# Down product of a two-stage expert network cut into chunks of 128 and 64 rows, five matmuls per tile instead of six

## The reference

```python
# layer 0: 64 experts, top 8 of 64 per token, softmax weights
gate = ragged_dot(hidden_sorted, gate_proj_w, group_sizes)      # 512 -> 192
up   = ragged_dot(hidden_sorted, up_proj_w, group_sizes)        # 512 -> 192
out  = ragged_dot(silu(gate) * up, down_proj_w, group_sizes)    # 192 -> 512
# layer 1: 48 experts kept of 128, top 8, at most 192 tokens per expert
g, u = split(einsum('ech,eoh->eco', xb, gate_up_proj), 2)
out  = einsum('eci,ehi->ech', silu(g) * u, down_proj)           # 192 -> 512
```

## Time and profile before

| | |
|---|---|
| median of 3 executions | 2465.17 us |
| the profiled execution | 2475.7 us |
| its span, first to last instruction | 2474.0 us |
| mean granted TensorE clock | 0.872 |
| first expert stage, first to last down product | 608.6 to 1284.6 us |
| second expert stage | 1985.2 to 2409.5 us |
| TensorE busy over the span | 1874.6 us, 76% |
| VectorE busy | 1669.7 us, 67% |
| GpSimd busy | 1318.0 us, 53% |
| ScalarE busy | 730.4 us, 30% |

### The profile page before, as it was taken

The page is one execution under the profiler, slowest core; times in us unless marked ns, Lnnn a source line. Parts: engine busy times, 40 slices in busy tenths (PEclk is TensorE's granted clock), DMA queues, the critical chain, the costliest instruction groups (busy, mean ns, idle before and its releaser), DMA issues. The chain is left out here.

```text
span 2474.0 us, 36661 instructions
## 1 busy us (share of the span) xinstructions
PE 1874.6 (76%) x9110; PEld 1485.2 (60%) x9111; DVE 1669.7 (67%) x2703; ACT 730.4 (30%) x1434; POOL 1318.0 (53%) x847
## 2 busy tenths in 40 slices
PE   6797969233999999999974979595702199999990
PEld 3464545122989988989973555353401188888880
DVE  5659676742767777777742276979697187787764
ACT  2121212001434444444432233333321034433440
POOL 2313656745777777777762000534343666677770
PEclk9898979565999999999996989798955599999995
DMA  6001021013887888888965102020100379988975
GB/s 237 17 18 51 1 68 35 1 64 94 208 216 196 219 230 220 233 227 231 243 123 198 34 1 85 0 85 1 52 0 34 100 201 235 239 228 227 241 157 209
DMA packets 126505, 325.18 MB, mean 131 GB/s; under 512 B 26636, under 2 KB 27148, under 8 KB 125042
## 3 DMA queue, kind: packets, MB, share of 16 engines
q0 software_dynamic: 68912, 124.93, 24.8%
q1 hardware_dynamic: 55426, 195.44, 23.9%
q10 hardware_dynamic: 2112, 4.19, 0.4%
HBM read 242.90 MB, written 99.45 MB: 138 GB/s over the span
## 5 line engine op out<-in xcount | busy, mean ns | idle before, releaser
L91 POOL DMA_INDIRECT tab_rows<-pair,slot x256 | 317.0, 1238 | 210.4 <-issue 101.7
L954 POOL DMA_INDIRECT xg<-x_rows,ids x270 | 374.0, 1385 | 100.3 <-issue 82.2
L83 PE MATMUL gu<-wgu_h,xgT_h 128*128 x1040 | 377.1, 363 | 6.5 <-DVE wgu_l L1108 2.7
L83 PE MATMUL gu<-wgu_l,xgT_h 128*128 x1040 | 354.5, 341 | 0.0
L83 PE MATMUL gu<-wgu_h,xgT_l 128*128 x1040 | 351.6, 338 | 0.0
L963 POOL DMA_INDIRECT acc_rows<-ysb,ids x128 | 228.2, 1783 | 129.5 <-DMA acc_rows<-ysb,ids 72.5
L963 POOL DMA_INDIRECT odd_rows<-ysb,ids x128 | 236.3, 1846 | 91.5 <-ACT ysb L1006 29.5
L1006 ACT ACTIVATE ysb<-yp,wts 128x512 f32<-128x512 f32 x256 | 176.5, 689 | 289.1 <-PE yp L83 240.4
L1123 DVE TENSOR_TENSOR xgT_l<-tpx,xgT_h 128x512 fp32r<-128x512 f32 x262 | 179.5, 685 | 110.8 <-ACT xgT_h L992 98.4
L83 PE MATMUL yp<-wd_h,hT_h 96*128 x512 | 222.6, 435 | 2.4 <-DVE hT_l L1131 1.9
L1108 DVE TENSOR_TENSOR wgu_l<-wgu_sb,wgu_h (+1 forms) x112 | 196.9, 1758 | 40.6 <-issue 39.8
(11 more groups left out here) (333 smaller groups left out, 3659.1 us busy)
## 6 DMA issues: line engine op xcount, KB each, us to landing
wgu_sb<-in_wgu SPq DMA_DIRECT2D x112, 768.0 KB
wd_sb<-in_wd SPq DMA_DIRECT2D x112, 384.0 KB
odd_rows<-zero SPq DMA_DIRECT2D x2, 4352.0 KB, 14.6
ct<-in_ctxT SPq DMA_DIRECT2D x8, 1024.0 KB, 4.9
xg<-x_rows,ids POOLq DMA_INDIRECT x270
xb<-in_x SPq DMA_DIRECT2D x4, 1024.0 KB
x_rows<-mag SPq DMA_DIRECT2D x4, 1024.0 KB, 4.4
acc_rows<-mag SPq DMA_DIRECT2D x4, 1024.0 KB, 6.7
```

What stands on the lines that cost most here:

```text
L83: i = nc.tensor.matmul(out, left(k), right(k), start=(start and k == 0 and m == 0), stop=(k == ops - 1 and m == 2))
L91: nc.gpsimd.indirect_dma_start(out=tab, out_offset=bass.IndirectOffsetOnAxis(ap=s["slot"][:, n:n + 1].bitcast(U32), axis=0), in_=s["pair"] ...
L954: nc.gpsimd.indirect_dma_start(out=xg[:, t % G, :], out_offset=None, in_=x, in_offset=bass.IndirectOffsetOnAxis(ap=ids[:, t:t + 1].bitcast ...
```

## The change

The contraction of 192 rows of the down product is cut into 128 + 64 instead of 96 + 96. For the first chunk the three products stay. For the chunk of 64 rows, columns 128 to 191 of h are written twice into h (columns 128 to 191 and 192 to 255), so that the transpose gives their upper part twice, on partitions 0 to 63 and 64 to 127. A weight tile wd_r holds the upper part of the 64 weight rows on partitions 0 to 63 and their lower part on 64 to 127. One matmul over 128 rows then makes upper x upper and upper x lower at once, and one over 64 rows makes lower x upper: 3 + 2 = 5. h gets a second VectorE product per tile, the weights a third transfer, and each split of the down weights is two instructions. The semaphore counts follow. Cut to its core, without the layout on the host (which now passes the down weights as rows, 192 per expert):

```diff
@@ -21,7 +21,7 @@
 HALF = D // 2
 TOPK = 8
 INTER = 192
-IC = 96
+IR = INTER - P
 E0, E1 = 64, 48
 EOLD = 128
 CAP = 192
@@ -822,18 +822,19 @@
         sb, ps, sem = alloc(nc, ctx)
 
         wgu = sb(f"wgu_sb{which}", [P, NR * KC, 2 * INTER])
-        wd = sb(f"wd_sb{which}", [IC, NR * 2, D])
+        wd = sb(f"wd_sb{which}", [P, NR * 2, D])
         wgu_h = sb(f"wgu_h{which}", [P, NB * KC, 2 * INTER], F32R)
         wgu_l = sb(f"wgu_l{which}", [P, NB * KC, 2 * INTER], F32R)
-        wd_h = sb(f"wd_h{which}", [IC, NB * 2, D], F32R)
-        wd_l = sb(f"wd_l{which}", [IC, NB * 2, D], F32R)
+        wd_h = sb(f"wd_h{which}", [P, NB, D], F32R)
+        wd_l = sb(f"wd_l{which}", [P, NB, D], F32R)
+        wd_r = sb(f"wd_r{which}", [P, NB, D], F32R)
         xg = sb(f"xg{which}", [P, G, D])
         xT_h = sb(f"xgT_h{which}", [P, 2, D], F32R)
         xT_l = sb(f"xgT_l{which}", [P, 2, D], F32R)
         sg = sb(f"sg{which}", [P, 2, INTER])
-        h = sb(f"h{which}", [P, 2, INTER])
-        hT_h = sb(f"hT_h{which}", [IC, 2, 2 * P], F32R)
-        hT_l = sb(f"hT_l{which}", [IC, 2, 2 * P], F32R)
+        h = sb(f"h{which}", [P, 2, 2 * P])
+        hT_h = sb(f"hT_h{which}", [P, 2, 2 * P], F32R)
+        hT_l = sb(f"hT_l{which}", [P, 2, 2 * P], F32R)
         ysb = sb(f"ysb{which}", [P, G, D])
         cnt = sb(f"cnt{which}", [ne, 1])
         cnti = sb(f"cnti{which}", [ne, 1], I32)
@@ -915,8 +916,9 @@
             def load(r, n):
                 e = sp.value_load(listed[0:1, bass.ds(r, 1)], min_val=0, max_val=ne - 1)
                 sp.dma_start(wgu[:, n * KC:(n + 1) * KC, :], wgu_d[bass.ds(e * P, P), :, :]).then_inc(s_wt, 16)
-                sp.dma_start(wd[:, n * 2:n * 2 + 2, :], wd_d[bass.ds(e * IC, IC), :, :]).then_inc(s_wt, 16)
-                sp.wait_ge(s_wt, r * 32 + 32)
+                sp.dma_start(wd[:, n * 2, :], wd_d[bass.ds(e * INTER, P), :]).then_inc(s_wt, 16)
+                sp.dma_start(wd[0:IR, n * 2 + 1, :], wd_d[bass.ds(e * INTER + P, IR), :]).then_inc(s_wt, 16)
+                sp.wait_ge(s_wt, r * 48 + 48)
                 settle(sp, passed)
 
             for n in range(NR):
@@ -928,7 +930,7 @@
 
                         sp.wait_ge(s_gl, (g - 1) * NR + (n + 1))
                         settle(sp, passed)
-                        sp.wait_ge(s_dl, (g - 1) * NR + (n + 1))
+                        sp.wait_ge(s_dl, (g - 1) * (NR * 2) + (n * 2 + 2))
                         settle(sp, passed)
                         load(g * NR + n, n)
 
@@ -997,7 +999,7 @@
 
             def copy_hT(t, q):
                 act.wait_ge(s_hT, t + 1)
-                nc.scalar.copy(hT_h[:, q, :], tph[0:IC, q, 0:2 * P]).then_inc(s_hTh, 1)
+                nc.scalar.copy(hT_h[:, q, :], tph[:, q, 0:2 * P]).then_inc(s_hTh, 1)
 
             def weighted(g, q, peeled):
                 act.wait_ge(s_y, g * G + q + 2)
@@ -1098,17 +1100,20 @@
 
                 raw, n = r % NR, r % NB
                 g_raw, g_up = wgu[:, bass.ds(raw * KC, KC), :], wgu_h[:, bass.ds(n * KC, KC), :]
-                d_raw, d_up = wd[:, bass.ds(raw * 2, 2), :], wd_h[:, bass.ds(n * 2, 2), :]
+                d_raw, d_rest, d_up, d_both = (wd[:, bass.ds(raw * 2, 1), :], wd[0:IR, bass.ds(raw * 2 + 1, 1), :],
+                                               wd_h[:, bass.ds(n, 1), :], wd_r[:, bass.ds(n, 1), :])
                 if part == 0:
-                    dve.wait_ge(s_wt, r * 32 + 32)
+                    dve.wait_ge(s_wt, r * 48 + 48)
                     nc.vector.tensor_copy(g_up, g_raw).then_inc(s_wh, 1)
                     nc.vector.tensor_copy(d_up, d_raw).then_inc(s_wh, 1)
+                    nc.vector.tensor_copy(d_both[0:IR], d_rest).then_inc(s_wh, 1)
                 elif part == 1:
-                    dve.wait_ge(s_wh, r * 2 + 2)
+                    dve.wait_ge(s_wh, r * 3 + 3)
                     nc.vector.tensor_tensor(wgu_l[:, bass.ds(n * KC, KC), :], g_raw, g_up.bitcast(F32), ALU.subtract).then_inc(s_gl, 1)
                 else:
-                    dve.wait_ge(s_wh, r * 2 + 2)
-                    nc.vector.tensor_tensor(wd_l[:, bass.ds(n * 2, 2), :], d_raw, d_up.bitcast(F32), ALU.subtract).then_inc(s_dl, 1)
+                    dve.wait_ge(s_wh, r * 3 + 3)
+                    nc.vector.tensor_tensor(wd_l[:, bass.ds(n, 1), :], d_raw, d_up.bitcast(F32), ALU.subtract).then_inc(s_dl, 1)
+                    nc.vector.tensor_tensor(d_both[IR:P], d_rest, d_both[0:IR].bitcast(F32), ALU.subtract).then_inc(s_dl, 1)
 
             def split_weights(r, first, part):
                 with dve.If(first > 0):
@@ -1124,11 +1129,12 @@
 
             def gated(t, q):
                 dve.wait_ge(s_sg, t + 1)
-                nc.vector.tensor_tensor(h[:, q, :], sg[:, q, :], gu[:, q, INTER:2 * INTER], ALU.mult).then_inc(s_h, 1)
+                nc.vector.tensor_tensor(h[:, q, 0:INTER], sg[:, q, :], gu[:, q, INTER:2 * INTER], ALU.mult).then_inc(s_h, 1)
+                nc.vector.tensor_tensor(h[:, q, INTER:2 * P], sg[:, q, P:INTER], gu[:, q, INTER + P:2 * INTER], ALU.mult).then_inc(s_h, 1)
 
             def split_hT(t, q):
                 dve.wait_ge(s_hTh, t + 1)
-                nc.vector.tensor_tensor(hT_l[:, q, :], tph[0:IC, q, 0:2 * P], hT_h[:, q, :].bitcast(F32), ALU.subtract).then_inc(s_hTl, 1)
+                nc.vector.tensor_tensor(hT_l[:, q, :], tph[:, q, 0:2 * P], hT_h[:, q, :].bitcast(F32), ALU.subtract).then_inc(s_hTl, 1)
 
             n_steps = steps_used(dve)
             r, f = ranks(dve, 0, G)
@@ -1198,20 +1204,23 @@
                         lambda k: wgu_l[:, bass.ds(n * KC + k, 1), :].rearrange("p a n -> p (a n)")).then_inc(s_gu, 1)
 
             def transpose_h(t, q):
-                pe.wait_ge(s_h, t + 1)
-                for k in range(2):
-                    i = nc.tensor.transpose(tph[0:IC, q, k * P:(k + 1) * P], h[:, q, k * IC:(k + 1) * IC], ident[:, :])
-                i.then_inc(s_hT, 1)
+                pe.wait_ge(s_h, t * 2 + 2)
+                nc.tensor.transpose(tph[:, q, 0:P], h[:, q, 0:P], ident[:, :])
+                nc.tensor.transpose(tph[:, q, P:2 * P], h[:, q, P:2 * P], ident[:, :]).then_inc(s_hT, 1)
 
             def down(t, q, r):
+
                 pe.wait_ge(s_hTl, t + 1)
-                pe.wait_ge(s_dl, r + 1)
+                pe.wait_ge(s_dl, r * 2 + 2)
                 pe.wait_ge(s_ye, t + 1)
                 n = r % NB
-                split_product(nc, yp[:, q, :], 2,
-                        lambda k: hT_h[:, q, k * P:(k + 1) * P], lambda k: hT_l[:, q, k * P:(k + 1) * P],
-                        lambda k: wd_h[:, bass.ds(n * 2 + k, 1), :].rearrange("p a n -> p (a n)"),
-                        lambda k: wd_l[:, bass.ds(n * 2 + k, 1), :].rearrange("p a n -> p (a n)")).then_inc(s_y, 1)
+                upper, lower, rest = (w[:, bass.ds(n, 1), :].rearrange("p a n -> p (a n)") for w in (wd_h, wd_l, wd_r))
+                nc.tensor.matmul(yp[:, q, :], hT_h[:, q, 0:P], upper, start=True, stop=False)
+                nc.tensor.matmul(yp[:, q, :], hT_l[:, q, 0:P], upper, start=False, stop=False)
+                nc.tensor.matmul(yp[:, q, :], hT_h[:, q, 0:P], lower, start=False, stop=False)
+                nc.tensor.matmul(yp[:, q, :], hT_h[:, q, P:2 * P], rest, start=False, stop=False)
+                nc.tensor.matmul(yp[:, q, :], hT_l[0:IR, q, P:2 * P], wd_r[0:IR, bass.ds(n, 1), :].rearrange("p a n -> p (a n)"),
+                                 start=False, stop=True).then_inc(s_y, 1)
 
             r, _ = ranks(pe, 0, 1)
             transpose_x(0, 0)
```

More of the change, by code:

```diff
@@ L1978, in layouts @@
         wgu0=gu0.reshape(E0, KC, P, 2 * INTER).transpose(0, 2, 1, 3).reshape(E0 * P, KC, 2 * INTER),
-        wd0=L0_ffn_down_proj_w.reshape(E0, 2, IC, D).transpose(0, 2, 1, 3).reshape(E0 * IC, 2, D),
+        wd0=L0_ffn_down_proj_w.reshape(E0 * INTER, D),
         wqkv=chunked(L1_attn_w_qkv.T), wo1=chunked(L1_attn_w_out.T), gate1=chunked(L1_ffn_gate_weight.T),
@@ L1983, in layouts @@
         wgu1=gu1.reshape(E1, KC, P, 2 * INTER).transpose(0, 2, 1, 3).reshape(E1 * P, KC, 2 * INTER),
-        wd1=L1_ffn_down_proj.transpose(0, 2, 1).reshape(E1, 2, IC, D).transpose(0, 2, 1, 3).reshape(E1 * IC, 2, D),
+        wd1=L1_ffn_down_proj.transpose(0, 2, 1).reshape(E1 * INTER, D),
     )
```

## The result

The changed kernel's median is 2497.8 us (2489.4 to 2505.8, 8 runs) beside 2466.6 us for the kernel before (2458.7 to 2481.4, 8 runs): ratio 1.0097, 95% interval 1.0061 to 1.0134. The change makes the program slower, by 15 to 33 us. The forecast was 2481 us, range 2440 to 2508; the time lies in it, 17 us above the forecast. The profiled spans are 2474.0 and 2497.1 us.

The account below looks back on a forecast made before the run. TensorE was taken to bound the first stage, the chain of weight loads the second. The terms -30 (TensorE) + 12 (given back) + 35 (loads) - 1 (last tiles) gave +16 us, forecast 2481 us, range 2440 to 2508.

Parts of the forecast that it names:

- second sentence on TensorE: Down product on TensorE: mixing 64 and 128 rows costs nothing, at worst 0.08 us per tile.
- The transposes: TensorE's two h transposes: 96 stationary columns become 128, 0.14 us becomes 0.18, plus 0.04 us per tile.
- The give-back in the first stage: First stage: 12 of the 30 us gained are lost again to the load chain and gathers; bounds 0 and 30.
- VectorE's work is covered: VectorE's added 0.2 us per tile, with h's second product at 0.15, hides behind TensorE's work of the tile.
- The 7.7 us for two tiles of VectorE's work: Consecutive two-tile experts: 4.6 us of splits and 2.9 of tile work reach about 7.7 beside TensorE's 7.9.
- The third transfer: Second stage: each expert's added transfer lands 0.8 us later, over 44 loads +35 us.
- "small price" rival: Third transfer costs 0.35 us per load, the two stages cancel, 2461 us; chance 0.31.
- the upper end: Landing price of the third transfer: 0.8 us, taken nearer 1.1 us per transfer than the lower bound 0.
- The gathers' 2.15 us per load: Load cycle 9.18 us against 7.03 before gathers begin; the difference read as 1.1 us per transfer.
- The full turn per load: Each load waits one turn of the gathers' queue, 1.3 us, 56 us over 44 loads, 2516 us; chance 0.10.
- bound by the chain of loads: Second stage paced by issue, landing, next issue: 44 cycles of 9.18 us against TensorE's 8.26 for two tiles.
- One of its signs: Second stage: SyncE's waits for wd_sb would rise by some 35 us.

Follow-up runs that it names:

- full-rows kernel: The changed kernel with the fifth down matmul over all 128 rows instead of 64, adding lower x lower; 2485.7 us beside 2477.6, ratio 1.0033.
- opened chain: The kernel before, with SyncE issuing the next expert's loads before waiting for the last landing; 2466.1 us, ratio 0.9962. On full rows with two transfers: 2459.3 us, ratio 0.9942.

## Why the prediction was right and where not

**The total** came out in the range and in the class with the largest chance, slower. But that is luck: in the profiles the first stage came out 26 us above its forecast (+8 instead of -18) and the second 22 below it (+12 instead of +34). Two errors of opposite sign nearly cancelled, and the cause of the slowdown was not the one forecast for the first stage.

**The step that failed** is the second sentence on TensorE: "That the last has 64 rows and the others 128 instead of 96 I cost at nothing", with 0.08 us as the worst. It cost 0.36 us. The argument was that the gap between matmuls stays one though the stationary operands alternate. The trace of before has operands of 96 and 128 rows only, between which nothing is paid, and I extended that to 64. The cost is no work of the matmul: the weight load is not pulled ahead of the one that runs. The text had a test for it (a floor above 3.98 says that mixing costs TensorE), and with 4.25 it struck. The first stage was forecast 18 us shorter and became 8 longer; without the mixing it is 12 shorter.

**The transposes** were charged +0.04 us. From the first transpose (1102.21, ahead of the lines shown) to the first down matmul (1102.35) it is 0.14 us as before, so +0.

**The give-back in the first stage** was 12 us with bounds 0 and 30. The full-rows kernel could gain 159 x 0.22 = 35 us and gains 12: 23 are given back, in the bounds. TensorE's waits for gathered rows rose from 9.3 to 18.9 us (weight loads) and from 5.1 to 6.2 (matmuls); the rest is not parted. In the changed kernel they fell to 2.7 and 0.8: with a floor of 4.25 the rows come in time. That VectorE's work is covered was right: 209 ns for the second product (0.15 taken, bounds 0.115 and 0.345), and its removal brings the first stage nothing. The 7.7 us for two tiles of VectorE's work do not come out of their terms (4.6 + 2.9 = 7.5), but no term of the sum hung on them.

**The third transfer** was the right mechanism with a wrong size: 0.8 us per load forecast, 0.26 in the change and 0.29 alone, near the "small price" rival. The choice of the upper end rested on the gathers' share of the queues, taken as a wait per transfer. The gathers' 2.15 us per load are hardly a price per transfer: a third one adds an eighth of that. The full turn per load (1.3 us) did not show. It was my reading of the Trainium skill's page (DMA: Bandwidth & Descriptors, "Queues, rings and completion order"). These runs refute that price; whether the rule itself holds, no run here shows.

**The second stage is bound by the chain of loads**: right, shown by full rows (no change there) and by the opened chain. One of its signs did not come: SyncE's attributed waits for wd_sb fell, 243.2 to 178.7 us in fewer entries, though the cycle grew. The distance between issues was the sound reading, the attributed wait was not.

## What to carry to other kernels

Counting matmuls is not enough: keep the row count of the stationary operands in one class, here by padding the last chunk to 128 rows, since a 64-row one among 128 saved nothing and stalled both itself and its successor. Only 64, 96 and 128 rows were tried: 96 and 128 went together, 64 did not. Where one queue issues, waits and issues again, the cycle (issue to issue) is the number to read; letting it run one load ahead gave 16 to 19 us in the second stage, as much as going from three transfers to two (17 us), and the two add up (437.5 to 420.3 to 401.1 us). A gain on the engine at the bound is worth what the next wait leaves of it, here a third.

## What the runs showed of the hardware

- A change between 128 or 96 rows and 64 costs 0.10 us before the 64-row matmul and 0.20 us behind it, with another 0.06 in the following transposes. A second 64-row matmul behind the first adds 0.23 in sum, like any of 512 columns, and its weight load is pulled ahead (1105.38 for a start at 1105.61); the gaps are then 0.34 and 0.32. The weight loads themselves last 0.18 and 0.19 us. The Trainium skill (TensorE: Matmul & The Clock Gate, "LDWEIGHTS (loading the stationary operand)") says that a load of fewer rows takes as long as one of 128; the trace agrees on the duration, and the cost lies in when the load may start.
- A 128-row float32 weight load does start under the running 128-row matmul (1102.89 under 1102.88).
- A third transfer with the same bytes and 45% more packets (15549 instead of 10752 in 400 us) adds 0.26 to 0.29 us to a load of 9.2 us that shares the engines with gathers; between the full-rows kernels with three and with two transfers it is 0.40 (9.51 and 9.11). Whether transfers or packets cost, and why no more, stays open.
